# Cross attention and mixture of experts on one core: another order of the key and value projections, wider GpSimd divisions, 71 expert tiles

## The reference, cut to what matters

```python
# x (8, 512, 512), ctx (8, 1601, 512); 16 heads of 32
x = x + xattn(layernorm(x), ctx, wq, bq, wkv, bkv, wp, bp)
x = x + ffn(layernorm(x), w_gate, wi_0, wi_1, wo)

# xattn
q = qdq(x) @ qdq(wq).T + bq                 # qdq: round to int8 steps and back
k, v = split(cond @ wkv.T + bkv, 2)         # 1601 keys and values for each sequence
attn = softmax(q @ k.T * scale)             # by head
out = qdq(attn @ v) @ qdq(wp).T + bp

# ffn: 8 experts, each token goes to its best 2
h0, h1 = ragged_dot(sorted_x, wi_0, sizes), ragged_dot(sorted_x, wi_1, sizes)
out_sorted = ragged_dot(silu(h0) * h1, wo, sizes)
out = weighted sum of a token's two rows
```

## Time and profile before

| | us |
|---|---|
| median of 3 runs (2184.74 to 2188.13) | 2186.44 |
| the profiled execution | 2184.58 |
| its span, first to last instruction | 2182.8 |
| PE busy | 1822.8 (84%) |
| DVE busy | 1795.8 (82%) |
| ACT busy | 1346.1 (62%) |
| POOL busy | 970.5 (44%) |
| attention, scores of the first to the last unit | about 135 to 1681 |
| routing | about 1700 to 1815 |
| experts | about 1815 to 2183 |

### The profile page before, as it was taken

How to read it: one execution, slowest core, us unless ns; L and a number is a source line. 1 busy time by engine, 2 the same in 40 slices (tenths; PEclk the granted TensorE clock), 3 DMA queues, 4 the chain that set the end, 5 groups by cost and what they waited for, 6 DMA issues and landing times. The chain is left out here.

```text
span 2182.8 us, 60639 instructions
## 1 busy us (share of the span) xinstructions
PE 1822.8 (84%) x24804; PEld 1263.3 (58%) x24804; DVE 1795.8 (82%) x2402; ACT 1346.1 (62%) x1944; POOL 970.5 (44%) x900
## 2 busy tenths in 40 slices
PE   1379998999989998999999898989996216999996
PEld 1247776666666666666666666667774102555553
DVE  4459989899999998999999999989988395666665
ACT  0347876777777777777777777778776332333332
POOL 0002553375256436534733653365334201676765
PEclk7679999999999999999999999999998557999998
DMA  2332331242233223313322332232221244566785
GB/s 87 94 87 51 88 109 34 82 111 80 65 93 104 77 77 92 101 48 89 105 80 65 100 92 75 75 96 78 56 58 32 92 146 138 177 199 220 244 265 169
DMA packets 152823, 225.40 MB, mean 103 GB/s; under 512 B 33861, under 2 KB 87109, under 8 KB 152545
## 3 DMA queue, kind: packets, MB, share of 16 engines
q1 hardware_dynamic: 130736, 166.89, 26.5%
q0 software_dynamic: 21808, 54.58, 8.1%
HBM read 131.37 MB, written 71.32 MB: 93 GB/s over the span
## 5 line engine op out<-in xcount | busy, mean ns | idle before, releaser
L764 DVE TENSOR_TENSOR a_p_low<-a_p 128x1024 f16<-128x1024 f32 (+1 forms) x896 | 1097.2, 1247 | 134.7 <-ACT a_p L642 125.7
L642 ACT ACTIVATE a_p<-ps_s 128x1024 f32<-128x1024 f32 (+1 forms) x896 | 862.1, 967 | 384.9 <-PE ps_s L493 377.5
L493 PE MATMUL ps_s<-a_q_stack,a_k_stack 96*128 96x512 f16 (+1 forms) x1664 | 515.9, 385 | 77.3 <-DMA a_k_stack<-a_k_parts 53.6
L604 PE MATMUL ps_o<-a_v,a_p 128*128 128x65 f16 (+1 forms) x6656 | 447.5, 194 | 19.6 <-ACT a_o_sums L668 9.5
L604 PE MATMUL ps_o<-a_v,a_p_low 128*128 128x65 f16 (+1 forms) x6656 | 447.7, 194 | 0.0
L526 PEld LDWEIGHTS ps_p<-wkv,a_ctx 128*128 128x128 f16 x4992 | 330.4, 99 | 165.7 <-DVE a_v L779 59.2
L526 PE MATMUL ps_p<-wkv,a_ctx 128*128 128x128 f16 x4992 | 379.3, 222 | 44.8 <-DVE a_v L779 44.5
L604 PEld LDWEIGHTS ps_o<-a_v,a_p 128*128 128x128 bf16 (+1 forms) x6656 | 352.1, 98 | 100.3 <-DVE a_p_low L764 24.5
L510 PE MATMUL ps_p<-a_ctx,wkv 128*128 128x384 f16 (+2 forms) x1536 | 349.1, 337 | 37.0 <-DVE a_ctx L402 34.3
L604 PEld LDWEIGHTS ps_o<-a_v,a_p_low 128*128 128x128 f16 (+1 forms) x6656 | 318.1, 98 | 0.0
L510 PEld LDWEIGHTS ps_p<-a_ctx,wkv 128*128 128x128 f16 x1536 | 148.4, 98 | 185.5 <-DVE a_ctx L402 31.0
(11 more groups left out here) (232 smaller groups left out, 2186.6 us busy)
## 6 DMA issues: line engine op xcount, KB each, us to landing
a_k_stack<-a_k_parts SPq DMA_DIRECT2D x384, 80.0 KB, 2.1
d_ys<-f_y SPq DMA_DIRECT2D x72, 256.0 KB
a_ctx_raw<-in_ctx_dram SPq DMA_DIRECT2D x64, 192.0 KB, 2.5
a_q_stack<-d_q_t SPq DMA_DIRECT2D x96, 128.0 KB, 3.5
a_xm<-in_x_dram SPq DMA_DIRECT2D x8, 1024.0 KB, 5.9
a_ctx_raw<-in_ctx_dram SPq DMA_DIRECT2D x32, 256.0 KB, 4.7
d_q_t<-a_q_parts SPq DMA_DIRECT2D x32, 256.0 KB, 2.7
d_q_full<-a_xm SPq DMA_DIRECT2D x32, 256.0 KB, 2.9
```

The source lines that it names most:

```text
L493: mm = pe.matmul(t["ps_s"][s % 2][0:r, n * N:(n + 1) * N], t["k_stack"][v % 2][0:TERMS * DH, j, kt * P:kt * P + r], t["q_stack"][v % 2][0: ...
L604: mm = pe.matmul(t["ps_o"][:, q * VC:(q + 1) * VC], part[0:r, n * N + q * P:n * N + (q + 1) * P], val, start=(g == 0 and n == 0 and low == ...
L642: act.activation(t["p"][s % NP][0:r, 0:len(tiles) * N], t["ps_s"][s % 2][0:r, 0:len(tiles) * N], ACT.Exp, scale=float(DH) ** -0.5 / WSCALE ...
L764: dve.tensor_tensor(t["p_low"][s % NP][0:r, 0:n], full, high, ALU.subtract).then_inc(lows, 1)
```

## The change

The eight jobs of a unit come in the order k0 k1 v0 k2 v1 k3 v2 v3, held in a list JOB_ORDER, by which the semaphore counts of DVE's low halves are also found. The jobs' ends become slots 4, 7, 11, 15, 18, 21, 24 and 27; the two stacks therefore stand at slots 18 and 24. The context of the next sequence is converted and loaded two slots later. On POOL the four additions of a normalisation are one instruction, and so are the four multiplications. TILES is 71, from the sum of the padded groups.

```diff
+JOB_ORDER = [("k", 0), ("k", 1), ("v", 0), ("k", 2), ("v", 1), ("k", 3), ("v", 2), ("v", 3)]
-TILES = 72
+TILES = (B * N * TOPK + E * (P - 1)) // P
...
-                    at = (NBLK * b - 2) * SLOTS + 12 + 7 * r + (0, 2, 3, 5)[c] if b else FIRST + 6 + 2 * (CC * r + c)
+                    at = (NBLK * b - 2) * SLOTS + 14 + 7 * r + (0, 2, 3, 5)[c] if b else FIRST + 6 + 2 * (CC * r + c)
...
-            new = [(kind, u, r) for r in range(4) for kind in "kv"]
+            new = [(kind, u, r) for kind, r in JOB_ORDER]
...
-                    at = FIRST + 18 + 6 * job[2] + (2 if job[0] == "v" else 0)
+                    at = FIRST + 18 + (0, 6, 8, 12, 14, 18, 20, 22)[new.index(job)]
...
-                dve.wait_ge(highs, 8 * u + 2 * r + 1)
+                dve.wait_ge(highs, 8 * u + JOB_ORDER.index(("k", r)) + 1)
...
-                for j in range(HB):
-                    last = pool.tensor_tensor(heads[:, j], sums[:, j, :, 0:DH], sums[:, j, :, DH:2 * DH], ALU.add)
-                out_done(last)
+                out_done(pool.tensor_tensor(heads, sums[:, :, :, 0:DH], sums[:, :, :, DH:2 * DH], ALU.add))
                 pool.wait_ge(inverted, v + 1)
-                for j in range(HB):
-                    last = pool.tensor_tensor(heads[:, j], heads[:, j],
-                                              t["o_inv"][:, v, j, :, None].to_broadcast([P, QT, DH]), ALU.mult)
-                out_done(last)
+                out_done(pool.tensor_tensor(heads, heads, t["o_inv"][:, v, :, :, None].to_broadcast([P, HB, QT, DH]),
+                                            ALU.mult))
```

More of the change, by code:

```diff
@@ L207 @@
 TT = B * N // P
-TILES = 72
-assert TILES * P >= B * N * TOPK + E * (P - 1)
+TILES = (B * N * TOPK + E * (P - 1)) // P
+assert B * N * TOPK % P == 0
 def group_tiles(g):
@@ L777, in values_low @@
                 v = t["v"][u % 2][:, tiles[0]:tiles[-1] + 1, :, :].rearrange("p t h c -> p (t h) c")
-                dve.wait_ge(highs, 8 * u + 2 * r + 2)
+                dve.wait_ge(highs, 8 * u + JOB_ORDER.index(("v", r)) + 1)
                 dve.tensor_tensor(v[:, :, DH:2 * DH],
@@ L1718, in _ @@
             for n in range(NY):
-                sp.wait_ge(y_out[n], 16 * (TILES // NY))
+                sp.wait_ge(y_out[n], 16 * len(range(n, TILES, NY)))
         @block.tensor
```

## The result

The changed kernel takes 2166.53 us (median of 4 runs, 2163.07 to 2166.77); the kernel before, run beside it, 2185.59 us (4 runs). The ratio is 0.9913, 95% interval 0.9891 to 0.9935: some 19 us faster where 35.5 were forecast. The time lies inside the range of 2122 to 2180, but 15.5 us above the forecast of 2151 and 1.5 us above the end of the 2138 to 2165 that the forecast claimed for itself. The profiled execution took 2163.07 us with a span of 2161.2.

What follows compares the result with a forecast made beforehand. In attention neither PE nor DVE was taken as the bound alone, each idling about 130 us. Terms -43 + 0 + 12 - 4.5 = -35.5 us, from the 2186.4 us median, gave 2151 us; range 2122 to 2180.

Steps and rivals of the forecast that it cites:

- Key order: Attention: stacking half 1 of the keys three slots earlier removes PE's wait for it; -43 us, ends -54 and -20.
- key wait: Attention: PE's wait for the transfers of the stacked keys, 53.6 us in 30 waits, forecast to go.
- What is queued behind on SP and POOL: Attention: context loads and stores come up to 8.6 us later, with some 10 us in hand; counted at nothing.
- Normalisation: POOL in attention: two long operations replacing eight short ones delay DVE's low halves; +12 us, range -16 to +50.
- Bank waits: Attention: PE's value jobs waiting for banks DVE had not freed, 44.5 us; change 0, 15 us to either side.
- Experts: Experts' stretch: one tile less of 72 saves one step, -4.5 us.
- Rival A: Attention: DVE binds throughout and fills the time PE no longer stands; -10 us, 2177 us; chance 0.20.
- B: Attention: both the key wait and the bank waits become time; -73 us, 2113 us; chance 0.17.
- C: Attention: long POOL operations hold DVE for all their length; slower, +32 us, 2219 us; chance 0.07.
- D: SP's queue: half 1 still lands late behind a context load waiting for POOL; only the tile's gain, 2182 us; chance 0.06.

Runs made afterwards that it cites:

- number 5: The changed kernel with the next sequence's context two slots earlier and eight short POOL operations instead of two long ones: 2142.48 us, ratio 0.9789 to the kernel before.
- 6: The kernel before with 71 tiles and the wait at the end that goes with it, nothing else: 2185.18 us, ratio 0.9982.
- number 1: The changed kernel with the next sequence's context two slots earlier, in the slots of the kernel before: 2175.94 us, ratio 0.979 to the kernel before.
- number 3: The kernel before with two POOL operations of 512 elements in place of eight of 128, nothing else: 2242.2 us, ratio 1.009.
- 7: Number 1 with a fifth raw buffer and all context splits ahead of the normalisation: 2139.96 us, ratio 0.9781 to the kernel before.
- 8: The kernel of 7 with eight short POOL operations instead of two long ones: 2145.67 us, ratio 0.9806 to the kernel before.
- 9: The changed kernel with only the third context range earlier, at slots 27, 28, 29 and 31: 2180.02 us, ratio 0.979 to the kernel before.
- 11: The changed kernel itself, run again in the last group beside 9: 2199.20 us, ratio 0.9879 to the kernel before.

## Why the prediction was right and where it failed

- **Key order: right in mechanism, and in size partly by luck.** The key wait is gone. -43 was forecast; numbers 5 and 6 give -42.7 (the difference of two medians on one chip, 9 us to either side by the intervals). It is a measure of the order with the context where it was. The agreement to 0.3 us is luck: in number 5 PE also stands 18.6 us in 6 waits for POOL's split of the context, a wait that the kernel before does not have and the forecast did not count, and DVE's wait for ACT fell to 95.8 us and not to 70 to 90.
- **What is queued behind on SP and POOL: this is the step that failed.** The prediction said that the context loads and stores come later and that "the context has six slots in hand before k1, k2 and k3 ask for it". That looked at the jobs that read the context. It did not walk the three queues that a moved piece passes: on POOL it moved behind the normalisation, and on SP the query stores stand behind its load, with ACT waiting for them. It was counted at nothing and costs 27 us by the ratios (0.9913 against 0.979), 19 us beside each other on one chip. The six slots did not hold for the readers either: PE waits 14.8 us for the split context in the changed kernel, in 6 waits, and 18.6 in number 1, where the context is two slots earlier. The prediction's own part on the change had asked the question for half 1 of the keys, and not for the context.
- **Normalisation: wrong in the kernel as changed, near in the one from which it was read.** +12 was forecast, +20 measured alone (number 3), inside the range, and it is DVE's time, as forecast. It does not lie where it was forecast, 0.4 us in every unit, but in the fourth unit alone, 53.7 us against 50.9, in which the normalisation of the unit before stands in slot 16 and not in slot 5. In the new order no cost shows (numbers 1 and 5, 7 and 8), so the term does not belong in this sum. The prediction priced the two parts one by one from a trace with the old order; they are not additive. Why stays open. The busy times of POOL (546 and 637 us) suggest which engine stands, not why, and no kernel was made that moves this normalisation.
- **Bank waits: 0, as counted.** PE's value jobs wait 14.6 and 11.9 us now, and 44.5 before, but other jobs wait more. These are the key jobs (L511), the gates (L569) and the output projection (L546):

```profile
PE ps_p L511 <- DVE a_k_parts L771: 8.5, 6, 1.6
PE ps_p L511 <- DVE a_v L780: 4.2, 6, 0.7
PE ps_p L569 <- DVE a_k_parts L771: 3.3, 6, 0.5
PE ps_p L546 <- DVE a_k_parts L771: 3.0, 1, 3.0
```

 All six rows make 45.5 us, within the 30 to 60 that were expected. The kernel before has 47.3 in such waits and number 5 has 50.4. So the waits moved and did not shrink, and none of the -42.7 is theirs.
- **Experts: right.** -4.5 forecast, -4.1 measured. The median step is as before, 4.55 us.
- **The sum.** With the measured terms: -42.7 + 0 + 0 - 4.1 = -46.8, and number 1, from another group, has 0.979, which is -45.9. From there to the result are the 27 us for the queue, but that number is the difference of just these two ratios, so a sum with it closes by itself. The group of numbers 9 and 11 gives the terms side by side: -46.6 without the queue fault and -27.4 with it. The changed kernel is thus 19 us faster than the one before in one group and 27 in another (ratios 0.9913 and 0.9879, whose intervals overlap), and the queue's price is known as 19 to 27 us. So the forecast of -35.5 was off by two errors of opposite sign: 12 counted for POOL that was not there, and 19 to 27 not counted for the queue. That the time lies in the range owes something to this.
- **Rival A** (2177, 2165 to 2181) has the time that came, but not its way: DVE is busy 1413.7 of 1537.4 us and idles 123.7, where it idled 127.2. Its sign, that DVE's idle time doesn't fall with PE's stall, came true for another reason, so the forecast was wrong by its own sign, and the sign alone could not tell A from this. B and C did not come, nor did D: half 1 landed in time, but the queue that D was afraid for is the one that failed, one line further on.
- **Other signs.** SP was to issue half 1 from slot 22 on; it issues it in slots 24 to 26, since its plan has it in slot 24, and that was early enough. The two POOL lines were to take 1.26 us at least. They do, nearly:

```profile
L905 POOL TENSOR_TENSOR a_o_full<-a_o_sums x32: 1282/1969/6956, 180.1 to 1672.3; 128x512 f32<-128x512 f32 x32
```

```profile
L907 POOL TENSOR_TENSOR a_o_full<-a_o_full,o_inv x32: 1047/1302/9378, 187.5 to 1673.7; 128x512 f32<-128x512 f32 x32
```

 The multiplication has a shorter one, 1047 ns. DVE's busy time was to rise by 5 to 20 us in attention; it is 1413.7 us and was 1419.0, so it did not rise.

A better kernel than both came out of the experiments: numbers 1, 5, 7 and 9, at 0.978 to 0.979 of before, are 0.9 to 1.2% faster than the change as it was made, and can't be told from one another.

## What to carry to other kernels

When a step moves, list for each of its instructions the engine's queue at the new place, what stands between the old place and the new one, and what stands behind it; a margin to the consumer of the data says nothing of the strangers in the queue, and it shrinks itself when the queue in between gets slower. A short run of tiny operations can be a long item in such a queue while the other engine is busy. And a cost read from a trace holds for that order: when one part of a change shifts who is idle when, the other parts have to be priced again.

## What the runs showed of the hardware

A POOL operation of 128x4 takes 0.20 us at least and 2.72 us beside two of DVE's low halves (the row of 1063.02 above); the longest in the changed kernel took 7.41 us, beside a row of eleven low halves:

```profile
1638.89 11.44 DVE L765 TENSOR_TENSOR a_p_low<-a_p 65x512 f16<-65x512 f32 x11
```

```profile
1638.98 7.41 POOL L916 TENSOR_TENSOR a_rstd_tmp<-a_rstd 128x4 f32<-128x4 f32 x1
```

So a short POOL operation can stand for several DVE operations that follow each other without a gap. Thirteen of them took 10.5 us in the unit above, and 5.1 in the kernel before. In the earlier trace rows and number 3 DVE was the one that took longer; here it is POOL, several operations in a row.

In the first and the last group the experts took 351 to 359 us instead of 313 to 320 in every kernel's trace (the kernel before took 36 to 41 us more in these groups too). The steps alternate there; ACT's last operation of a tile in number 1:

```profile
1901.52 0.68 ACT L1785 ACTIVATE f_y<-f_py,slot_weight 128x512 f32<-128x512 f32 x1
1905.83 0.68 ACT L1785 ACTIVATE f_y<-f_py,slot_weight 128x512 f32<-128x512 f32 x1
1911.84 0.68 ACT L1785 ACTIVATE f_y<-f_py,slot_weight 128x512 f32<-128x512 f32 x1
```

Steps of 4.3 and 6.0 us, where number 5 has 4.55 throughout. PE waits 1 us for DVE's `f_xt` in the long ones. Why it is so in two groups and not in the others stays open.
